# Attention scores on TensorE: four 128x128 blocks a row of the batch become eight 64x64 blocks in two column groups

## What is computed

```python
h = _layernorm(x) * (1 + ca) + sa
qkv = h @ w_qkv + b_qkv                                   # q, k, v: (B, H, L, 64)
scores = einsum('bhld,bhle->bhde', q, k) / sqrt(64)       # 64x64 a head
attn = softmax(scores, axis=-1)
out = einsum('bhld,bhde->bhle', v, attn) ... @ w_fc + b_fc
x = x + ga * _layernorm(out + h) ...                      # then gamma, beta
h = _layernorm(x) * (1 + cb) + sb
xr, xk = mixes of h with h one step earlier               # mu_r, mu_k
x = x + gb * sigmoid(xr @ W_r.T) * (relu(xk @ W_k.T)**2 @ W_v.T)
```

## Time and profile before

| | us |
|---|---|
| median of 3 runs | 707.26 |
| lowest, highest | 706.86, 707.5 |
| span of the profiled execution | 704.2 |
| TensorE (PE) matmuls busy | 676.1 (96%) |
| weight loads (PEld) busy | 548.0 |
| VectorE (DVE) busy | 524.8 (75%) |
| ScalarE (ACT) busy | 392.8 (56%) |
| GpSimd (POOL) busy | 389.5 (55%) |

### The profile page before, as it was taken

The page is one execution under the profiler, slowest core; times in us unless marked ns, Lnnn a source line. Parts: engine busy times, 40 slices in busy tenths (PEclk is TensorE's granted clock), DMA queues, the critical chain, the costliest instruction groups (busy, mean ns, idle before and its releaser), DMA issues.

```text
span 704.2 us, 11623 instructions
## 1 busy us (share of the span) xinstructions
PE 676.1 (96%) x3584; PEld 548.0 (78%) x3584; DVE 524.8 (75%) x1030; ACT 392.8 (56%) x871; POOL 389.5 (55%) x809
## 2 busy tenths in 40 slices
PE   7988999999999999999999999999999999998896
PEld 6767787978788887887879787888878878786665
DVE  4784898768878687868877688786878588467853
ACT  1434575556655475474755565554754747546552
POOL 5172885567275663586455672756635864326530
PEclk9999999999999999999999999999999999999999
DMA  9759255675846375573926657563755629616225
GB/s 317 220 166 210 90 158 91 130 163 113 194 86 146 120 158 118 97 177 89 217 77 133 162 117 184 89 151 111 165 116 92 124 57 199 117 29 153 30 31 89
DMA packets 90984, 93.02 MB, mean 132 GB/s; under 512 B 4224, under 2 KB 89000, under 8 KB 90960
## 3 DMA queue, kind: packets, MB, share of 16 engines
q0 software_dynamic: 33264, 33.03, 31.9%
q1 hardware_dynamic: 55344, 55.97, 24.9%
q10 hardware_dynamic: 2352, 3.73, 1.5%
HBM read 42.84 MB, written 33.10 MB: 108 GB/s over the span
## 4 chain that ended last, share of the span: by engine, by line
PE 34%; POOL 26%; issue 21%; DVE 9%; ACT 6%; DMA 2%; POOLq 1%; DVEq 0%; SPq 0%
PE work L1307 6%; PE att L1274 5%; PE gram L1256 5%; PE work L1324 4%; POOL x L483 4%; POOL ag L461 2%; ACT z L699 2%; POOL wv_aug L494 2%; PE tr L1249 2%; POOL ag_a L461 2%; DVE t_buf L894 2%; DVE mx L923 2%; POOL wv_aug L497 2%; PE gram L1385 2%; POOL rs_o L478 2%
## 5 line engine op out<-in xcount | busy, mean ns | idle before, releaser
L1274 PE MATMUL att<-m_sb,z_t 128*128 128x256 f32 x496 | 112.9, 381 | 8.4 <-DVE t_buf L894 7.6
L1274 PEld LDWEIGHTS att<-m_sb,z_t 128*128 128x128 f32 x496 | 92.4, 190 | 24.9 <-issue 13.7
L1324 PE MATMUL work<-mx,w_k_t 128*128 128x512 f32 x236 | 106.2, 592 | 0.0
L1307 PE MATMUL work<-w_r_t,mx 128*128 128x256 f32 x464 | 105.0, 379 | 0.0
L894 DVE SCALAR_TENSOR_TENSOR t_buf<-att,rs_o,g_row 128x256 f32<-128x256 f32 x124 | 51.4, 477 | 64.4 <-POOL rs_o L478 64.4
L1307 PEld LDWEIGHTS work<-w_r_t,mx 128*128 128x128 f32 x464 | 86.1, 190 | 10.4
L699 ACT ACTIVATE z<-x,ag 128x256 f32<-128x256 f32 x128 | 66.5, 598 | 48.6 <-POOL ag L471 48.6
L1256 PE MATMUL gram<-z 128*128 128x256 f32 (+1 forms) x512 | 89.7, 329 | 0.0
L449 POOL TENSOR_TENSOR ag<-st 128x4 f32<-128x4 f32 x32 | 18.6, 582 | 125.5 <-DVE st L905 125.5
L652 ACT ACTIVATE sq<-att 128x256 f32<-128x256 f32 x124 | 45.9, 382 | 72.4 <-PE att L1274 72.4
L1256 PEld LDWEIGHTS gram<-z 128*128 128x128 f32 x512 | 80.4, 192 | 6.7
(11 more groups left out here) (176 smaller groups left out, 1373.8 us busy)
## 6 DMA issues: line engine op xcount, KB each, us to landing
x_in<-in_L_attn_x_dram SPq DMA_DIRECT2D x32, 512.0 KB, 4.9
x<-rows SPq DMA_DIRECT2D x32, 512.0 KB, 3.5
x<-in_L_attn_x_dram POOLq DMA_DIRECT2D x32, 512.0 KB, 9.4
out_dram<-x SPq DMA_DIRECT2D x31, 512.0 KB, 4.8
out_dram<-y POOLq DMA_DIRECT2D x29, 512.0 KB, 6.0
rows<-row_scratch SPq DMA_DIRECT2D x16, 128.0 KB, 4.9
rows<-row_scratch SPq DMA_DIRECT2D x8, 256.0 KB, 3.8
wqkv_sb<-in_L_attn_w_qkv_dram ACTq DMA_DIRECT2D x1, 1536.0 KB, 10.0
```

Of the source, the lines that this page charges most:

```text
L1274: ins = mm(att_banks(j, alone)[q][:, (t % 2) * D:(t % 2 + 1) * D], z_t[:, j, k, t * P:(t + 1) * P], m_sb[:, k], start=(k == 0), stop=(k == ...
L1307: ins = mm(r_banks(alone)[q][:, (t % 2) * D:(t % 2 + 1) * D], mixed(j, alone)[0][:, ch, tile], w_r_t[:, ch], start=(ch == 0), stop=(ch == ...
L1324: ins = mm(k_banks(alone)[dh][:], w_k_t[:, ch, rows_dh], mixed(j, alone)[1][:, ch], start=(ch == 0), stop=(ch == KD - 1))
```

## The change

Each pair of heads is made as two products, one a head: head g of the pair uses 64 columns of weights (its channels of `gq`) and 64 moving columns (its channels of the key weights), and its 64x64 block goes to partitions 64g to 64g + 63 of `gram`. The partitions of the output decide which column group of the array works, so g = 0 is in columns 0 to 63 and g = 1 in columns 64 to 127. The blocks off the diagonal are no longer made. The number of products goes from 8 to 16 per row. Nothing else differs: the same semaphore is raised by the last product.

```diff
                 for p in range(NP):
                     for m in range(KD):
-                        ins = mm(gram[:, p * P:(p + 1) * P], gq[:, m, p * P:(p + 1) * P], wqk_aug[:, m, HD + p * P:HD + (p + 1) * P],
-                                 start=(m == 0), stop=(m == KD - 1))
+                        for g in range(2):
+                            lo = p * P + g * DX
+                            ins = mm(gram[g * DX:(g + 1) * DX, lo:lo + DX], gq[:, m, lo:lo + DX],
+                                     wqk_aug[:, m, HD + lo:HD + lo + DX], start=(m == 0), stop=(m == KD - 1))
                 ins.then_inc(score_done, 1)
```

## The result

The changed kernel takes 703.06 us (median of 10 runs, 701.96 to 704.69); the kernel before, run beside it, 706.76 us (10 runs, 705.11 to 708.2). The ratio is 0.995 with a 95% interval of 0.9935 to 0.9965. It is 0.5% faster where I forecast 0.5% slower. The predicted range held the time, since it reached to the rival that came true: the two column groups work side by side, for which I had 703.2 us.

The account below looks back on a forecast made before the run. PE's own work was taken to bound the kernel, 81 of 82 us a row. (0.08 + 0.34) x 8 = 3.4 us slower took the median from 707.26 to 710.6 us; the 8-in-10 range was 702.6 to 712.4.

Parts of the forecast that it names:

- What bounds the kernel, and the path: Loop row: PE's own work fills 81 of 82 us, and time changed in the scores moves the row one for one.
- The `t_buf` stall: PE's one wait in a loop row, before an `attention`: about 1.0 us, claimed to stay and absorb no change.
- The rate of a 64x64 record: Scores on PE: 32 records one after the other at 58 ns, 1.86 us against 1.78, +0.08 us a pass.
- the side-by-side rival: Scores on PE: both column groups stream at once, -0.51 us a pass with entry and return, 703.2 us; chance 0.30.
- Going into column groups and back: Around the scores on PE: shape changes and exposed weight loads on entering and leaving cost +0.34 us a pass.
- the first rival: Scores on PE: the two column groups work side by side, 4.1 us faster in all, 703.2 us; chance 0.30.
- The second rival: Scores on PE: only some pairs overlap, 706.9 us, or no change of shape, 707.9 us; chance 0.12 together.
- The third: Scores on PE: each step between groups costs 0.14 us, 727 us; chance 0.10 including a flat 0.111 us a record.

Follow-up runs that it names:

- e6: The changed kernel with every pass making its sixteen products twice, the second time onto the same blocks: 710.02 us, 1.0061 of the kernel before.
- e3b: The changed kernel with both heads' blocks put into column group 0, scores left incomplete, for timing alone: 709.0 us, 1.0038 of the kernel before.
- e4: The changed kernel with each product 128 moving columns wide, so blocks off the diagonal are made again: 709.11 us, 1.0038 of the kernel before.
- e2: The changed kernel with products issued two and two (A A B B) instead of alternating (A B A B): 703.56 us, 0.9964 of the kernel before.
- e1: The changed kernel with all eight products of head g = 0 first, then all eight of g = 1: 707.59 us, 1.0027 of the kernel before.
- e7: The changed kernel with four column groups of 32 weight columns, two products for each head: 702.08 us, 0.9949 of the kernel before.
- e9: The changed kernel with the start-up's products of 128 weight and 8 moving columns also made in two column groups: 703.74 us, 0.9972 of the kernel before.

## Why the prediction was wrong

- **What bounds the kernel, and the path**: right. PE's own work sets the row; e6 put 0.94 us into the pass and the row grew by 0.95. The `t_buf` stall stayed.
- **The rate of a 64x64 record**: this is the step that failed. Both slopes were right (138 and 222 ns, 58 ns a record in one group, as e3b measured), but I multiplied 58 ns by 32 where it holds for 16 pairs. I took "+0.08 us a pass" where two groups give -0.85 (e4 against the change). What led me there was the argument against the side-by-side rival: loads start in order, each with the matmul before it, "so loads in order already fill the time". All rows for that were of one group. They show the order within a group, and say nothing of two. At its own price the rival was right: -0.51 us a pass, and a row is 0.53 shorter.
- **Going into column groups and back**: right. I had 0.34 from rows of 8-column weights; e4 shows 0.31, and the parts are there: 0.20 instead of 0.12 before the first record, 0.11 for the first pair instead of 0.06, 0.15 from the last start to `ffn_r` instead of 0.06, and 3.72 instead of 3.62 for `ffn_r`. The Trainium skill, "TensorEngine Tiling (Array Packing)", Key Properties, says that a change of tiling mode drains the engine, not of the tile in it: the trace agrees, with 0.31 us for a visit and none for the 15 steps between the groups inside.
- **Rivals**: the first came true; its sum was 703.2 and the median 703.06. The closeness has some luck: I counted eight passes, and the gain of the start-up's is not seen, so 7 x 0.53 = 3.7 instead of 4.1. I had also left the clock alone, and in the start-up it was not the same in the two profiles. The second rival is out for this order of issue: the pairs overlap wholly, and e4 pays for the shape. Part of the overlap is lost only when the order is another (e2, e1). The third (each step from group to group costs 0.14 us) is out: pairs start within 10 ns. The skill's "TensorE: Matmul & The Clock Gate", Part 3, which I had set beside the first rival with 0.30, was the better guide: it states that each further tile, in column groups too, starts some 4 ns behind the one before, and the trace agrees in that a pair starts within 10 ns. By its measured gain of 2.38 for three groups I should have given that case more.
- The same page's Part 1 was no limit either. Its 62 ns of sequencer time for each matmul is not seen: in e7 they follow each other every 14 ns on average, which is also under the 25 ns that it gives as the least distance between starts. Within one group the distance was 58 ns (e3b).

## What to carry to other kernels

A product of which only diagonal blocks are used can be made block by block in column groups at half the time, if the groups alternate in the order of issue; groups in turn (e1) or blocks in one group (e3b) are slower than the whole product. Going into the groups and back costs about 0.3 us for float32 weights of 128 columns behind it, so a visit must save more than that: here 0.85. Groups do not speed up full products whose moving side sets the rate (e4), but they do where the weight load sets it (e9: 1.71 to 0.91 us), and then it must be seen that PE is what others wait for.

## What the runs showed of the hardware

- Float32 products in two column groups stream and load weights side by side: pairs of records every 58 ns at 64x64, and in four groups of 32 columns, 64 records in 0.88 us.
- Two groups overlap only where their records stand near each other in the order of issue: four of a kind in a row cost 0.05 us a pass (e2), and at a seam between stretches of sixteen the time saved is that of three records (e1).
- A change of the array's shape costs 0.09 us beyond the rate, each way, and the first loads behind it are exposed, 0.05 us for 64 columns and 0.10 for 128.
